# Attention with high and low parts: the two 128-column products of the low weights taken over 256 columns

## What is computed

```python
qkv = silu(hidden_states @ qkv_w.T)          # per head: q, k, v of 128 features
def step(kv, blk):
    cq, ck, cv = blk
    scores = einsum('bhnd,bhmd->bhnm', cq, ck) * diag_decay
    intra = einsum('bhnm,bhmd->bhnd', scores, cv)
    inter = einsum('bhnd,bhde->bhne', cq * q_decay, kv)
    kv_next = kv * block_decay + einsum('bhnd,bhne->bhde', ck * k_decay, cv)
    return (kv_next, intra + inter)
```

## Time and profile before

| | us |
|---|---|
| median of 3 runs | 1056.68 |
| lowest, highest | 1054.97, 1058.63 |
| the profiled execution | 1056.38 |
| its span in the profile | 1054.6 |
| PE (TensorE matmuls) busy | 1014.6 |
| PEld (weight loads, beside PE) busy | 884.8 |
| DVE busy | 790.9 |
| ACT busy | 667.7 |
| POOL (GpSimd) busy | 376.3 |

### The profile page before, as it was taken

The page is one execution under the profiler, slowest core; times in us unless marked ns, Lnnn a source line. Parts: engine busy times, 40 slices in busy tenths (PEclk is TensorE's granted clock), DMA queues, the critical chain, the costliest instruction groups (busy, mean ns, idle before and its releaser), DMA issues.

```text
span 1054.6 us, 15829 instructions
## 1 busy us (share of the span) xinstructions
PE 1014.6 (96%) x5690; PEld 884.8 (84%) x5690; DVE 790.9 (75%) x1095; ACT 667.7 (63%) x1092; POOL 376.3 (36%) x347
## 2 busy tenths in 40 slices
PE   6889999999999999999999999999999999998996
PEld 4778898889988898889988898888988898886784
DVE  7467878679767878679767878679767878678767
ACT  5457864778647864777647864777647874766433
POOL 6424414332324414332323414332323414300565
PEclk9889999999999999999999999999999999998998
DMA  4111111112111111112112102112112102111302
GB/s 154 40 53 58 46 33 59 48 39 71 45 49 58 45 32 60 43 43 71 46 46 60 45 29 63 40 46 70 46 40 66 46 26 65 41 45 41 112 1 80
DMA packets 49006, 55.46 MB, mean 53 GB/s; under 512 B 4256, under 2 KB 41504, under 8 KB 48928
## 3 DMA queue, kind: packets, MB, share of 16 engines
q1 hardware_dynamic: 48928, 54.44, 16.4%
HBM read 52.33 MB, written 2.10 MB: 52 GB/s over the span
## 4 chain that ended last, share of the span: by engine, by line
PE 85%; DVE 9%; issue 2%; POOL 2%; ACT 1%; DMA 0%; SPq 0%; POOLq 0%; DVEq 0%; ACTq 0%
PE ps L1484 20%; PE ps L1485 19%; PE ps L1486 19%; PE ps L1478 8%; PE ps L1479 7%; PE ps L1480 7%; PE ps L1602 1%; PE ps L1587 1%; DVE s L849 1%; DVE wl L868 1%; DVE wl L849 1%; DVE xl L849 1%; DVE yl L849 1%; PE ps L1604 1%; PE ps L1589 1%
## 5 line engine op out<-in xcount | busy, mean ns | idle before, releaser
L1484 PE MATMUL ps<-xh,wh 128*128 128x512 f32 x672 | 270.4, 402 | 12.6 <-DVE wl L849 8.6
L1485 PE MATMUL ps<-xl,wh 128*128 128x512 f32 x672 | 265.1, 395 | 0.0
L1486 PE MATMUL ps<-xh,wl 128*128 128x512 f32 x672 | 264.1, 393 | 0.0
L1399 POOL TENSOR_TENSOR stage<-stage 128x512 f32<-128x512 f32 x64 | 93.1, 1455 | 344.2 <-DMA stage<-stream 344.2
L1419 POOL TENSOR_TENSOR sqacc<-sqacc,sq 128x512 f32<-128x512 f32 x64 | 92.4, 1444 | 289.2 <-ACT sq L503 289.2
L849 DVE TENSOR_TENSOR wl<-stage,wh 128x768 fp32r<-128x768 f32 (+3 forms) x149 | 165.9, 1123 | 37.0 <-ACT wh L350 37.0
L1484 PEld LDWEIGHTS ps<-xh,wh 128*128 128x128 f32 x672 | 127.7, 190 | 39.6 <-issue 9.9
L350 ACT ACTIVATE wh<-stage 128x768 fp32r<-128x768 f32 (+3 forms) x149 | 125.5, 855 | 53.6 <-PE ps L1480 33.7
L1486 PEld LDWEIGHTS ps<-xh,wl 128*128 128x128 f32 x672 | 127.7, 190 | 27.8
L1485 PEld LDWEIGHTS ps<-xl,wh 128*128 128x128 f32 x672 | 128.2, 191 | 23.0
L1484 PE MATMUL ps<-wh,xh 128*128 128x256 f32 x448 | 129.4, 289 | 5.2 <-DVE wl L849 5.2
(11 more groups left out here) (142 smaller groups left out, 2189.4 us busy)
## 6 DMA issues: line engine op xcount, KB each, us to landing
stage<-stream SPq DMA_DIRECT2D x64, 384.0 KB, 3.3
stage<-stream SPq DMA_DIRECT2D x36, 256.0 KB, 2.8
stage<-stream SPq DMA_DIRECT2D x66, 128.0 KB, 2.1
dec<-decay SPq DMA_DIRECT2D x32, 128.0 KB, 2.0
acc<-xt SPq DMA_DIRECT2D x4, 512.0 KB, 5.9
stage<-x SPq DMA_DIRECT2D x8, 256.0 KB, 4.2
out<-acc SPq DMA_DIRECT2D x8, 256.0 KB, 2.0
stg<-lora_router SPq DMA_DIRECT2D x1, 288.0 KB, 3.0
```

The costliest lines, as they stand in the source:

```text
L1399: nc.gpsimd.tensor_tensor(stage[:, s, 1:5:3, :], stage[:, s, 0:6:5, :], stage[:, s, 7:8, :].broadcast_to([P, 2, U]), ALU.add).then_inc(t_p ...
L1484: nc.tensor.matmul(dst, wt[0], mv_[0], start=start, stop=False, skip_group_check=True)
L1485: nc.tensor.matmul(dst, wt[0], mv_[1], start=False, stop=False, skip_group_check=True)
L1486: return nc.tensor.matmul(dst, wt[1], mv_[0], start=False, stop=stop, skip_group_check=True)
```

## The change

In the scores the product with the low keys takes the high and the low queries side by side, 256 columns in place of 128, so that low x low is added. In the attention the product with the low values of the second 128 tokens takes the high and the low scores side by side, 256 columns in place of 128. The three matmuls of the first 128 tokens are written out, and the third of them (low values x high scores, 256 columns) moves to the end, where it raises att_done.

```diff
                     nc.tensor.matmul(ps[:, S_B + b, SEQ:W], kh[:, q0 + P:q0 + SEQ], q2[:, :, q0 + P:q0 + SEQ],
                                      start=True, stop=False)
-                    last = nc.tensor.matmul(ps[:, S_B + b, SEQ:SC], kl[:, q0 + P:q0 + SEQ], qh[:, q0 + P:q0 + SEQ],
+                    last = nc.tensor.matmul(ps[:, S_B + b, SEQ:W], kl[:, q0 + P:q0 + SEQ], q2[:, :, q0 + P:q0 + SEQ],
                                             start=False, stop=True)
                 last.then_inc(sc_done, 1)
...
                     bank = ps[:, S_B + b, :]
-                    mm3(bank[:, 0:SEQ], (vh[:, 2 * b, :], vl[:, 2 * b, :]),
-                        (sh[:, b, 0:SEQ], sl[:, b, 0:SEQ]), True, False)
-
-
+                    nc.tensor.matmul(bank[:, 0:SEQ], vh[:, 2 * b, :], sh[:, b, 0:SEQ], start=True, stop=False)
+                    nc.tensor.matmul(bank[:, 0:SEQ], vh[:, 2 * b, :], sl[:, b, 0:SEQ], start=False, stop=False)
                     nc.tensor.matmul(bank[:, P:SC], vh[:, 2 * b + 1, :], s2[:, :, b, SEQ:SC],
                                      start=False, stop=False, skip_group_check=True)
-                    last = nc.tensor.matmul(bank[:, P:SEQ], vl[:, 2 * b + 1, :], sh[:, b, SEQ:SC],
-                                            start=False, stop=True)
+                    nc.tensor.matmul(bank[:, P:SC], vl[:, 2 * b + 1, :], s2[:, :, b, SEQ:SC],
+                                     start=False, stop=False, skip_group_check=True)
+                    last = nc.tensor.matmul(bank[:, 0:SEQ], vl[:, 2 * b, :], sh[:, b, 0:SEQ], start=False, stop=True)
                 last.then_inc(att_done, 1)
```

## The result

| | before | after |
|---|---|---|
| median of 20 runs each, us | 1055.46 | 1059.13 |
| lowest, highest, us | 1053.81, 1059.80 | 1057.78, 1061.05 |
| ratio after / before (95% interval) | | 1.0034 (1.0025 to 1.0043) |
| span of the profiled execution, us | 1054.6 | 1058.6 |

The kernel became slower by 0.34%. I had forecast +0.19% with a time of 1058.7 us, and had given "slower by over 0.3%" a chance of 0.25. The time lies in the range; the mechanism is the one forecast, and the size of its main term was read too small.

A forecast was written before the change was run, and what follows sets the result against it. PE (TensorE) was taken to bound the kernel. Widened matmuls +2.0, later signals +0.1 and time given back -0.1 sum to +2.0 us; from the median 1056.68 that makes 1058.7 us (+0.19%), range 1055.8 to 1062.2 us.

The forecast's parts named there:

- PE bounds, and the middle passes every added nanosecond on: Between start and tail, nearly every nanosecond added to PE's stream adds to the time; 0.26 us per middle group.
- The short matmul waits for the next weight load: Scores, 128-column matmul: weight loads set a floor of 0.1115 us, so its missing 128 columns buy almost nothing.
- The price of a widened matmul: Scores and attention: each of 256 widened matmuls costs 0.008 us, +2.0 us in all.
- 144-column row: Row of 144-column matmuls in PE's trace, 13 distances averaging 0.1115 us, taken as the weight-load floor.
- upper price: Most a widened matmul could cost: 0.0085 us (2.2 us in all) from the floor; one score block allowed 2.6 us.
- The signals: Last matmuls of scores and attention signal other engines some 0.06 us later, 64 of each; +0.1 us.
- the order: Attention: moving the vl product with the first half's sh from third to fifth of five matmuls costs nothing.
- What is given back: Groups 1 to 7: two widened matmuls each run in PE's waiting time beside a DVE chain; -0.1 us.
- Rival A: All widened matmuls: added columns wholly hidden, +0, 1056.7 us; chance 0.14.
- Rival B: All 256 widened matmuls: columns cost in full, 0.06 us each, 15.4 us, 1072.1 us; chance 0.06.
- Rival C: Scores and attention: later signals reach PE through 38 waits, 2.3 us on top of 2.0, 1061.0 us; chance 0.10.
- Rival D: Mainly the tail: another number of PE half-clock stretches; one gone 1055.3, two gone 1052, one more 1062.1 us; chance 0.10.

The follow-up runs named there:

- the order alone: Kernel before, still 128 columns, with the short matmul moved ahead in both scores and attention so a 256-column one is last; ratio 0.9991, repeated 0.9996.
- the order undone: Changed kernel, both products widened, but the products with vl keep their old places in attention, so the widened one is last; ratio 1.0030, 1059.16 us.
- all three comparisons: The unedited changed kernel measured three times against the kernel before; ratios 1.0034, 1.0031 and 1.0023.

## Why the prediction was right, and what was off

- *PE bounds, and the middle passes every added nanosecond on.* Right: a group grew by 2.04 / 6 = 0.34 us, where I had said 0.26. The only waits of PE between 85 and 955 us are still those for yl, 0.8 us in place of the 1.8 of the earlier trace rows:

```profile
PE ps L1478 <- DVE yl L849: 0.8, 2, 0.6
```

- *The short matmul waits for the next weight load, so that its missing columns buy almost nothing.* That the columns buy almost nothing is shown. Four widths now stand in the same block of ten (second start after it, minus first start, in ns over the score blocks between matmuls of 256 columns):

| columns of the two matmuls | block, us | step per matmul, ns |
|---|---|---|
| 64 | 1.294 | |
| 128 | 1.300 | +3 for 64 columns |
| 256 | 1.320 | +10 for 128 columns |
| 384 | 1.425 | +52 for 128 columns |

From 64 to 256 columns a floor sets the pace and 192 columns cost 13 ns; from 256 to 384 each column costs 0.41 ns, that is one cycle of 2.4 GHz. The kernel before stood on the flat part, the changed kernel stands near its end: if the last 10 ns below 256 are also paid at 0.41 ns a column, the flat part ends some 24 columns below 256, an estimate that no width between 128 and 256 has tested. That the floor is the weight load is argued and not shown, since every matmul here has its load of 128 x 128 and no run changes one; for it speaks that the loads keep their even step while the matmuls' starts don't. The prediction's sentence on the load "of the next but one" is weaker than the rows: it is already the load of the next matmul that never starts before the current matmul does (52.59 and 52.59 in the earlier trace rows, and 1 ns later at the least over all 5690), and the load after it follows 0.11 us later.

- *The price of a widened matmul, taken as 0.008 us.* This is the step that was off: **"I take 0.008 us, near the 144-column row because that is an average over 13 distances"**. It measured 10 ns in the blocks and 10.4 in the stream, 2.6 to 2.7 us in place of 2.0, so that even the 0.0085 us that I had called an upper price was too low. The 144-column row gave a floor of 0.1115 us, but the short matmul with its 128 columns and its successor together take 0.230 us, which leaves 0.110 for the short one. My upper price for a block, 0.01 us each or 2.6 us, was nearly the truth. The 1.31 us of the one block was 1.300 in nanoseconds, and against 1.320 that is 10 ns for each of the two. A median over many blocks would have given it in the trace of before; I had looked at one block, with starts printed to 0.01 us.
- *The signals, +0.1 us, and the order, 0.* Right within what can be measured, about 1 us; the order alone and the order undone show it. The later end was 0.07 us, not 0.06.
- *What is given back, -0.1 us.* Not separated. With 384 columns the output projection took 1.6 us less than in the changed kernel, so the direction is right.
- *Rival A, wholly hidden.* Wrong: all three comparisons exclude 1.000. *Rival B, full price.* Wrong at 256 columns by a factor of six, and near from 256 to 384, 52 ns where it has 60. The Trainium skill's gap of N / 2.4 + 2.5 ns ("TensorE: Matmul & The Clock Gate", "Back-to-back issue gap") gives the slope above 256 columns, where the trace agrees with 52 ns for 128 columns, and not below. The same page of the Trainium skill has, in its section "LDWEIGHTS", P / 1.2 ns for P columns, which makes 107 ns for 128 columns, an estimate near the floor of 110 ns here. *Rival C* fell with the order alone, and by what is left beside the columns, 0.5 us. *Rival D*: the stretches at low clock do differ from execution to execution, at the start in the kernel before as well. In the tail the one from about 960 us lasts 6.8 us in both profiles of before and 3.4 us in all three of the changed kernel, but 6.8 us again in the one with the order undone, whose median time is the same. From the second mark to the end the two profiles of before have 179.6 and 178.7 us, the three of the changed kernel 180.0, 179.9 and 179.9, of which 28 widened matmuls explain 0.3. So some tenths of a us may come from the tail, and this stays open.
- *The chances.* 0.71 for "within 0.3%" against 0.25 for slower: with the right price of 2.6 to 2.7 us the forecast would have been 0.25%, and the two cases should have stood close to even.

## What to carry to other kernels

A matmul record that got shorter is no gain; take the distance from the start before it to the second start after it, over many blocks and in nanoseconds, and compare it with the distance between full neighbours. Where every matmul loads 128 columns of weights of this 4-byte type, the columns that move through the array cost 13 ns in all from 64 to 256 and 0.41 ns each from 256 to 384. So the product low x low of the second 128 tokens, 128 columns more in 256 matmuls, is had here for 0.3%; what it does to the result was not measured. And narrowing a single matmul below that width gains next to nothing. Taking away a matmul together with its weight load should gain, but no run here tries it.

## What I had not expected

The floor isn't quite flat: 64 columns fewer still give back 3 ns each (1.294 against 1.300 us), although the weight loads seem to stand at an even step, and although the matmuls of a single column in the tail stand 112 ns apart. I leave the cause open.

The kernel's noise is at its two ends. Six groups of heads repeat within 0.4 us (712.96 and 712.57 before; 715.00, 714.92 and 714.80 after), and within 0.13 us without the output projection, while 20 whole executions of the kernel before spread over 6 us. For an effect of 0.3% that lies in the stream, two marks in the middle of one profile, with the waits between them set apart, say more than a dozen times.

Without that, two marks mislead: widening one product alone seemed to add less in the six groups than half of what both add, 713.37 us with the scores alone and 712.80 with the attention alone, against 712.96 before and 715.00 with both. The waits for yl took it back. Between the marks they are 1.0 us in the first profile of before and none in those two, and without the output projection each product adds its 0.95 us. Why the waits for yl differ, also between two profiles of the kernel before (1.8 and 0.9 us from 85 to 955 us), stays open.
